# The quantised last layer moved into the second attention's block, with its row scaling on ScalarE and its final sums on GpSimd

## What is computed

```
amax  = max|x|                                  over all 2048 tokens
scale = min(448 / max(amax, 1e-12), 448)        the same for the weight
x_fp8 = clip(x * scale, -448, 448) as float8_e4m3
acc   = x_fp8 @ w_fp8.T
out   = bfloat16(acc * (1/x_scale) * (1/w_scale) + bias)
h     = h + float32(out)
```

## Time and profile before

| what | value |
|---|---|
| median of three runs | 820.75 us (820.22 to 821.57) |
| the profiled execution | 825.86 us, its span 824.0 us |
| busy: TensorE, VectorE, ScalarE, GpSimd | 88%, 55%, 42%, 15% of the span |
| granted TensorE clock, mean | 0.923 |
| last instruction of the second attention's block | ends at 782.82 us |
| first instruction of the tail | 786.76 us |
| last VectorE instruction of the tail | ends at 821.45 us |

### The profile page before, as it was taken

How to read it: one execution, slowest core, us unless ns; L and a number is a source line. 1 busy time by engine, 2 the same in 40 slices (tenths; PEclk the granted TensorE clock), 3 DMA queues, 4 the chain that set the end, 5 groups by cost and what they waited for, 6 DMA issues and landing times. The chain is left out here.

```text
span 824.0 us, 15994 instructions
## 1 busy us (share of the span) xinstructions
PE 723.3 (88%) x5608; PEld 574.6 (70%) x5608; DVE 450.3 (55%) x1136; ACT 349.0 (42%) x596; POOL 121.6 (15%) x166
## 2 busy tenths in 40 slices
PE   5687899999889999999999999996788998887546
PEld 4566677677767999999999999984455665564212
DVE  4455767767764442353222332233787778865677
ACT  2232453244324212221112222317588978898213
POOL 2010112221222030000001001003323321111000
PEclk8789999999998999999999999999789988989855
DMA  5969675376358466555555655646367534660002
GB/s 162 190 111 246 64 84 80 57 102 83 64 72 272 172 227 238 180 166 189 186 185 196 191 178 198 176 108 97 58 82 103 88 66 54 77 77 1 1 13 89
DMA packets 70710, 102.66 MB, mean 125 GB/s; under 512 B 8160, under 2 KB 58472, under 8 KB 70512
## 3 DMA queue, kind: packets, MB, share of 16 engines
q1 hardware_dynamic: 67504, 93.34, 50.9%
q0 software_dynamic: 3136, 8.40, 3.5%
HBM read 63.88 MB, written 12.58 MB: 93 GB/s over the span
## 5 line engine op out<-in xcount | busy, mean ns | idle before, releaser
L1841 PEld LDWEIGHTS psum<-arena 128*128 128x128 f32 x1248 | 144.9, 192 | 1.9
L1841 PE MATMUL psum<-arena 128*128 128x128 f32 x1248 | 146.1, 275 | 0.0
L1892 PE MATMUL psum<-arena 128*128 x624 | 141.3, 379 | 0.8 <-DVE arena L1390 0.8
L846 ACT ACTIVATE arena<-psum,arena 128x128 f32<-128x128 f32 x156 | 44.5, 368 | 194.5 <-PE psum L1841 114.9
L1892 PEld LDWEIGHTS psum<-arena 128*128 128x128 f32 x624 | 115.5, 190 | 15.3 <-issue 1.2
L1803 PE MATMUL psum<-arena 96*128 96x256 bf16 x512 | 84.3, 299 | 26.4 <-ACT arena L817 15.2
L1803 PEld LDWEIGHTS psum<-arena 96*128 96x128 bf16 x512 | 47.0, 103 | 62.5 <-ACT arena L817 27.2
L1372 DVE TENSOR_SCALAR arena<-psum,arena 128x128 f32<-128x128 f32 x156 | 43.9, 344 | 81.1 <-PE psum L1841 66.4
L1244 DVE TENSOR_TENSOR arena<-arena 128x1024 f32<-128x1024 f32 x64 | 80.0, 1315 | 5.5 <-ACT arena L816 3.5
L817 ACT ACTIVATE arena<-psum,neg_mu 128x1024 f32<-128x1024 f32 x64 | 68.8, 1119 | 14.0 <-PE psum L1803 8.3
L1390 DVE TENSOR_TENSOR arena<-psum,arena 128x256 f32<-128x256 f32 x39 | 16.6, 425 | 96.2 <-PE psum L1892 96.2
(11 more groups left out here) (293 smaller groups left out, 1155.3 us busy)
## 6 DMA issues: line engine op xcount, KB each, us to landing
arena<-in_L_ffn_w_dram SPq DMA_DIRECT2D x47, 1024.0 KB, 5.1
arena<-arena SPq DMA_DIRECT2D x192, 128.0 KB, 5.7
arena<-xg SPq DMA_DIRECT2D x39, 128.0 KB, 2.0
yg<-arena SPq DMA_DIRECT2D x39, 128.0 KB, 1.7
out_dram<-arena SPq DMA_DIRECT2D x8, 256.0 KB, 2.1
xg<-zeros SPq DMA_DIRECT2D x9, 128.0 KB, 2.7
arena<-in_x_dram SPq DMA_DIRECT2D x8, 128.0 KB, 7.1
arena<-in_L_ffn_b_dram SPq DMA_DIRECT2D x1, 1024.0 KB, 12.2
```

What stands on the lines that cost most here:

```text
L846: ins = act.activation(hidT[:, v, c, :], psum[:, 2 * v, c * P:(c + 1) * P], ACT.Relu, bias=b1c[:, v, c:c + 1])
L1841: mm = pe.matmul(psum[:, 2 * v + c // HALF, (c % HALF) * P:(c % HALF + 1) * P], w1b[:, i % W1_BUFS, d, c * P:(c + 1) * P], xtT[:, v, d, :] ...
L1892: mm = pe.matmul(y_bank, hidT[:, u, c, :], w2s[:, one(e), c, :].rearrange("p o n -> p (o n)"), start=(c == 0), stop=(c == HC - 1))
```

## The change

The tail's code is moved from its own block to the end of each engine's stream in the second attention's block, and the last block is gone. On VectorE the tail now waits for the last update of amax through its semaphore. Four things are otherwise done:

- ScalarE makes two scaled copies of a batch's x3 before VectorE needs them (scaled, L946 and L947 of the new code): f_up, by scale times 2^20, and f_y, by the scale. Both have two buffers. It runs two batches ahead: scaled(b + 2) waits until f_q of batch b is written, and stands ahead of turned_out(b) in the stream.
- quantise(b) has three steps: the exponent of f_up is masked and a half bit set (L1569), its maximum with a constant is added to f_y (L1571), and the same maximum is taken less that sum, as bf16 (L1575); this is the rounded value with its sign turned, and scale_o has a minus to turn it back. The clips at plus and minus 448 are left out.
- rounded(b) is on VectorE (L1584): PSUM times scale_o plus the bias, which is read as float32 and repeated over the two tiles, rounded to bf16. No bias goes through TensorE, and the steps that split it are gone.
- The final sum h plus f_o is on GpSimd (L730), with the wait for the output transfer of batch b - 2.

```diff
-        scale_b = carve([1], F32, 4)
-        bias_row = carve([D], F32, 4)
-        bias_rest = carve([D], F32, 4)
-        bias_parts = carve([3, D], BF16, 2)
-        f_y = carve([QT, D], F32, 4)
+        scale_up = carve([1], F32, 4)
+        f_y = carve([2, QT, D], F32, 4)
+        f_up = carve([2, QT, D], F32, 4)
         f_e = carve([QT, D], I32, 4)
...
-        SCALE_STEPS = 8
-        BIAS_STEPS = SCALE_STEPS + 1 + 4 + 2
+        SCALE_STEP = 6
+        BACK_STEP = SCALE_STEP + 2
+        UP = 2.0 ** 20
+        HALF_BIT = 1 << 22
+        GRID = 1.5 * UP * 2.0 ** -6
...
+        def over_rows(v):
+            return v.rearrange("p (o d) -> p o d", o=1).to_broadcast([P, QT, D])
...
+                for b in range(B):
+                    sp.wait_ge(S["f_out"], b + 1)
+                    sp.dma_start(out[b].rearrange("(q p) d -> p q d", p=P), f_out[:, b % 2]).then_inc(o_out[b % 2], 16)
+                for u in range(2):
+                    sp.wait_ge(o_out[u], 16 * B // 2)
...
+                for b in range(B):
+                    pool.wait_ge(S["f_o"], b + 1)
+                    if b >= 2:
+                        pool.wait_ge(o_out[b % 2], 16 * (b // 2))
+                    pool.tensor_tensor(f_out[:, b % 2], h[:, b * QT:(b + 1) * QT, :], f_o[:, b % 2], ALU.add).then_inc(S["f_out"], 1)
...
+                def scaled(b):
+                    if b >= 2:
+                        act.wait_ge(S["qz_q"], b - 1)
+                    x = x3[:, b * QT:(b + 1) * QT, :].rearrange("p q d -> p (q d)")
+                    act.activation(f_up[:, b % 2].rearrange("p q d -> p (q d)"), x, ACT.Copy, scale=scale_up).then_inc(S["f_y"], 1)
+                    act.activation(f_y[:, b % 2].rearrange("p q d -> p (q d)"), x, ACT.Copy, scale=scale_x).then_inc(S["f_y"], 1)
+                def turned_out(b):
+                    act.wait_ge(S["fT_mm"], b + 1)
+                    if b >= 2:
+                        act.wait_ge(S["f_mm"], b - 1)
+                    act.copy(f_qT[:, b % 2].rearrange("p c t -> p (c t)"), psum[:, 2 + b % 2, 0:T].bitcast(BF16)
+                             ).then_inc(S["fT_done"], 1)
+                act.wait_ge(S["q_step"], SCALE_STEP)
+                scaled(0)
+                scaled(1)
+                for b in range(B):
+                    if b + 2 < B:
+                        scaled(b + 2)
+                    turned_out(b)
...
+                def settle_scale(ins):
+                    q_steps[0] += 1
+                    ins.then_inc(S["q_step"], 1)
+                    dve.wait_ge(S["q_step"], q_steps[0])
+                dve.wait_ge(S["am_done"], 2 * B)
+                settle_scale(dve.tensor_reduce(amax_x, amax[:, 1], AX, ALU.max))
+                dve.wait_ge(S["am_mm"], 1)
+                settle_scale(dve.tensor_reduce(amax_x, psum[:, 0, 0:P], AX, ALU.max))
+                settle_scale(dve.tensor_scalar(amax_x, amax_x, 1e-12, None, ALU.max))
+                settle_scale(dve.reciprocal(scale_i, amax_x))
+                settle_scale(dve.tensor_scalar(scale_x, scale_i, FP8_MAX, FP8_MAX, ALU.mult, ALU.min))
+                settle_scale(dve.tensor_scalar(scale_up, scale_x, UP, None, ALU.mult))
+                assert q_steps[0] == SCALE_STEP
+                settle_scale(dve.reciprocal(scale_i, scale_x))
+                settle_scale(dve.scalar_tensor_tensor(out=scale_o, in0=scale_i, scalar=-1.0, in1=w8s[:, 3:4], op0=ALU.mult, op1=ALU.mult))
+                assert q_steps[0] == BACK_STEP
+                def quantise(b):
+                    u = b % 2
+                    dve.wait_ge(S["f_y"], 2 * b + 1)
+                    settle_scale(dve.tensor_scalar(f_e, f_up[:, u].bitcast(I32), EXPONENT, HALF_BIT, ALU.bitwise_and, ALU.bitwise_or))
+                    dve.wait_ge(S["f_y"], 2 * b + 2)
+                    settle_scale(dve.scalar_tensor_tensor(out=f_t, in0=f_e.bitcast(F32), scalar=GRID, in1=f_y[:, u],
+                                                          op0=ALU.max, op1=ALU.add))
+                    if b >= 2:
+                        dve.wait_ge(S["fT_mm"], b - 1)
+                    dve.scalar_tensor_tensor(out=f_q[:, u], in0=f_e.bitcast(F32), scalar=GRID, in1=f_t,
+                                             op0=ALU.max, op1=ALU.subtract).then_inc(S["qz_q"], 1)
+                    dve.wait_ge(S["qz_q"], b + 1)
+                def rounded(b):
+                    u = b % 2
+                    dve.wait_ge(S["f_mm"], b + 1)
+                    if b >= 2:
+                        dve.wait_ge(S["f_out"], b - 1)
+                    dve.scalar_tensor_tensor(out=f_o[:, u], in0=psum[:, 4 + u, :].rearrange("p (q d) -> p q d", q=QT), scalar=scale_o,
+                                             in1=over_rows(ffn_b[:]), op0=ALU.mult, op1=ALU.add).then_inc(S["f_o"], 1)
+                for b in range(B):
+                    quantise(b)
+                    if b >= 2:
+                        rounded(b - 2)
+                rounded(B - 2)
+                rounded(B - 1)
...
-        with nc.Block() as block:
-            @block.sync
-            def _(sp):
...
-                def turn(b):
+                def turned_rows(b):
                     u = b % 2
                     pe.wait_ge(S["qz_q"], b + 1)
                     if b >= 2:
...
                     u = b % 2
                     if b >= 2:
                         pe.wait_ge(S["f_o"], b - 1)
-                    for i in range(3):
-                        pe.matmul(psum[:, 4 + u, :].rearrange("p (q d) -> p q d", q=QT), onesb[0:1, :],
-                                  over(bias_parts[0:1, i, :], 1, [1, QT, D]), start=(i == 0), stop=False)
                     pe.wait_ge(S["fT_done"], b + 1)
                     for q in range(QT):
                         for c in range(DC):
                             mm = pe.matmul(psum[:, 4 + u, q * D:(q + 1) * D], f_qT[:, u, c, q * P:(q + 1) * P],
-                                           fqT[:, c, :], start=False, stop=(q == QT - 1 and c == DC - 1))
+                                           fqT[:, c, :], start=(c == 0), stop=(c == DC - 1))
                     mm.then_inc(S["f_mm"], 1)
-                turn(0)
-                pe.wait_ge(S["q_step"], BIAS_STEPS)
+                turned_rows(0)
                 for b in range(B):
                     if b >= 1:
-                        turn(b)
+                        turned_rows(b)
                     product(b)
```

More of the change, by code:

```diff
@@ L333, in tower_kernel @@
             m_stat m_mv m_eps m_rstd x3_done am_done
-            w8_in w8_step w8_mm w8_done q_step am_mm b_parts qz_q fT_mm fT_done f_mm f_o f_out""".split()
+            w8_in w8_step w8_mm w8_done q_step am_mm f_y qz_q fT_mm fT_done f_mm f_o f_out""".split()
         scat = [sem(f"scat{u}") for u in range(2)]
@@ L1505, in _ @@
                 all_batches(iteration)
+                q_steps = [0]
+                def settle_scale(ins):
[6 more added lines that the diff above has]
+                settle_scale(dve.tensor_reduce(amax_x, psum[:, 0, 0:P], AX, ALU.max))
@@ L1983, in _ @@
                 all_batches(iteration)
-        with nc.Block() as block:
-            @block.sync
-            def _(sp):
[L1990 to L2054, removed]
-                    dve.tensor_tensor(f_q[:, b % 2], f_t, f_e.bitcast(F32), ALU.subtract).then_inc(S["qz_q"], 1)
-                    dve.wait_ge(S["qz_q"], b + 1)
[L2058 to L2062, removed]
-                    dve.tensor_tensor(f_out[:, u], h[:, b * QT:(b + 1) * QT, :], f_o[:, u], ALU.add).then_inc(S["f_out"], 1)
-                for b in range(B):
-                    quantise(b)
-                    if b == 0:
-                        split_bias()
-                    if b >= 2:
-                        finish(b - 2)
-                finish(B - 2)
-                finish(B - 1)
-            @block.tensor
-            def _(pe):
```

## The result

| | kernel before | changed kernel |
|---|---|---|
| median | 823.86 us (20 runs, 820.22 to 828.48) | 818.32 us (20 runs, 813.14 to 823.42) |
| ratio | 1 | 0.9932, 95% interval 0.9914 to 0.9951 |
| profiled execution | 825.86 us, span 824.0 us | 817.57 us, span 815.7 us |
| the tail: from the end of the last amax update to the span's end | 41.2 us | 36.7 us |
| of it behind the end of quantise(7) | 7.0 us | 11.1 us |

What follows compares the result with a forecast made beforehand. VectorE's stream was taken to bound the tail, apart from a barrier stall and the end. Barrier -3.9, start -4.0, periods +0.2 and end +1.35 make -6.35 us off 820.75: 814.4 us, range 809.3 to 817.3 (8 in 10).

Steps and rivals of the forecast that it cites:

- What bounds the kernel: Last 41 us: VectorE busy 29.46 of 41.00 us; a barrier, a start, five equal periods of its stream and an end.
- The barrier: Between last amax update and first tail step: one block gives back 3.94 - 0.04 = 3.9 us.
- The start: From the tail's first step to the end of quantise(2): 12.7 us becomes 8.7, a gain of 4.0 us.
- The five periods: Middle of the tail: 2.59 us own work plus 0.95 GpSimd hold, 3.54 for 3.50 us; 0.2 us lost in all.
- both of the cases that I read: In the attention, one GpSimd addition cost VectorE 0.87 us starting first, 0.97 us when VectorE started first.
- The first rival: Tail periods: GpSimd's sums don't block VectorE; period 2.59 us, 4.75 us more won, 809.6 us; chance 0.10.
- the second: Five periods: GpSimd blocks VectorE for the whole addition, 1.25 us for 0.95; 1.5 us more, 815.9 us; chance 0.10.
- The end: Behind quantise(7): batch 7's sum waits for batch 5's output buffer; 8.35 us against 7.0, 1.35 us lost.
- Sum: Whole tail: -3.9 - 4.0 + 0.2 + 1.35 = -6.35 us, giving span 817.6 and median 814.4 us.
- The reference point: Whole kernel: the 6.35 us were taken off the shown runs' median of 820.75 us.
- The third rival: Ahead of the tail: the 3.94 us belong to something at its start that stays, not the barrier; 818.3 us; chance 0.05.
- The fourth rival: Tail sums: GpSimd's bf16 to float32 addition is dear; at twice the price, 2.5 us, 823.2 us; chance 0.05.

Runs made afterwards that it cites:

- Experiment 7: Changed kernel with sums of batches 5 to 7 on VectorE and GpSimd filling f_out with zeros for batches 0 to 4; period 2.57 us, tail 28.42 us.
- experiment 8: Changed kernel with GpSimd's sums of batches 0 to 3 started beside rounded(b + 1), the other four on VectorE; tail 30.95 us, ratio 0.9878 to the kernel before.
- Experiment 5: Changed kernel with a DRAIN added on GpSimd in the attention's round 5, behind its last indirect transfers; tail 33.58 us, ratio 0.9887 to the kernel before.
- experiment 6: Changed kernel with a DRAIN added on GpSimd near the start, behind the constants and ahead of all its indirect transfers; tail 36.59 us, one run.

## Why the prediction was wrong

The forecast was 814.4 us with a range of 809.3 to 817.3; the median is 818.32. The direction was right, and so was the mechanism in the five periods, the barrier's 3.9 us (not their reason) and the start to 0.15 us. The periods won 0.5 us where I had 0.2 lost, and the end was 2.7 us too cheap. By the prediction's own steps:

- **What bounds the kernel.** Right up to quantise(7): in the middle of the tail VectorE's stream runs without a gap, and it still does. At the very end it is GpSimd's DRAIN now.
- **The barrier, -3.9 us.** The 3.9 us went, 0.03 us are left. The reason was wrong in part: I took the stall for the price of the barrier and wrote that the other engines had long been idle. GpSimd's queue wasn't: it was in its DRAIN until 786.4. I had read the instructions that count as busy, and what the rows name as the releaser (TensorE's queue), but not the queues' own rows of the line L453.
- **The start, -4.0 us.** 8.58 us measured for 8.7, and 12.73 before: -4.15. A copy of ScalarE took 0.71 to 0.72, not 0.74.
- **The five periods, +0.2 us.** 3.40 for 3.54, so -0.48 for the five. Own work 2.57 (2.59 expected). The hold is 1.52 - 0.69 = 0.83 us, below both of the cases that I read (0.87 and 0.97). The first rival (no blocking) and the second (the whole addition, 1.25) are both out. By the Trainium skill's rule (SBUF — State Buffer, Who interferes with whom) the pair is held for the whole instruction. Experiment 7 agrees on who is in the way of whom. I had priced the rule at the addition's whole 1.25 us, and that was wrong: the sum starts beside the exponent step, and when f_t starts (798.97) 0.97 us of it are left (to 798.68 + 1.26 = 799.94). f_t lost 0.83, 0.14 less than that. In experiment 8 0.61 us are left when the exponent step starts and 0.46 are lost, 0.15 less. In the kernel before, where L700 starts first, 1.12 us were left and 0.87 lost. So what VectorE loses is the rest of GpSimd's instruction at the time its own could start, less 0.14 to 0.25 us, and 0.83 against 1.26 says nothing against the rule.
- **The end, +1.35 us.** The step that failed. The wait for batch 5's output buffer was there as forecast, 1.12 us ahead of the last sum, and the last sum ended 5.4 us behind quantise(7) for 5.8. But "behind the last sum 2.55 us as now" was wrong: it took 5.7, for GpSimd's DRAIN. The piece measured 11.08 - 7.01 = +4.07 us, 2.7 more than I had put. Experiment 5 adds one DRAIN in the attention and leaves the tail's instructions alone: 3.14 us go, 7.94 us are left behind quantise(7) with 2.54 behind the last sum. The other 0.93 us are the buffer's wait and the sums, for which I had 1.35.
- **Sum.** -3.91 - 4.15 - 0.48 + 4.07 = -4.47 us against the forecast -6.35: 1.9 us of the tail's gain weren't there.
- **The reference point.** I took the sum off the three runs shown, 820.75 us. The median of twenty is 823.86, so 3.1 us of the miss are not in the change at all; from that median my -6.35 would have given 817.5, and the tail's -4.47 gives 819.4. So of the 3.9 us between forecast and median 3.1 are the reference point's and 1.9 the tail's, and by 1.1 the medians show more than the tail, within the scatter named above. The profiled execution at 825.86 us had been a hint that the three runs were on the fast side; the range names the spread of runs, but with no figure, and left 2.9 us above the forecast for everything.
- **The third rival** (the 3.94 us belong to something that stays; 0.05, 818.3 us) came nearest. Its mechanism as put (code loading at the start of the tail) was wrong, but its core holds, that the stall isn't the barrier's: what caused it came back at the end, for 3.1 us (experiment 5). That its 818.3 us is the measured median is luck, since it too was counted from 820.75; from the median of twenty it would be 821.4.
- **The fourth rival** (a dear mixed addition) is out: 1.26 us beside VectorE, 1.15 alone.

## What to carry to other kernels

When a stall stands at a block's end, ask for the closing instructions of every queue, also of those that show no work: the one with the long DRAIN is the one to look at, and the releaser that a view names may be another, as TensorE's queue was here. Where an engine has issued indirect transfers, try a DRAIN of its own in an idle stretch before its last work: here one instruction was worth 3.1 us. Before a step goes from VectorE to GpSimd, set what VectorE saves against what GpSimd's reads take from the instructions beside it: here 0.73 us saved and 0.83 lost a batch, and it paid only beside an instruction that reads PSUM (0.46 lost). And take the reference from as many runs as the change will be measured with.

## What the runs showed of the hardware

- GpSimd's DRAIN lasted 5.4 to 5.5 us beyond its last arithmetic when the engine had issued indirect transfers since its last DRAIN, even 32 us after the last of them (experiment 5), and 0.05 to 0.1 us when it had issued none. Behind two ordinary transfers at the start it took 9.6 us in all and ended 0.1 us behind the landing of the second (experiment 6).
- A float32 sum of 128x512 on GpSimd held VectorE's step with two SBUF inputs for 0.83 us, where 0.97 us of the sum were left, and the single-input exponent step for 0.46 us, where 0.61 were left; an exponent step that had started before the sum kept its 0.42 us. A fill of the same size (0.73 us) held the two-input step for nothing. The sum didn't hold an instruction that reads PSUM and one SBUF operand (0.75 us either way); no fill ran beside one.
- GpSimd added bf16 to float32 at the price of float32 alone: 1.26 us beside VectorE's work, 1.15 where VectorE was reading PSUM or idle.
- The same kernel before had medians of 823.8, 824.2 and 834.0 us in three sessions (15, 11 and 7 runs; the third on another chip than the first two), while the tails of the changed kernel and of the version of experiment 8 repeated to 0.05 us.
